# Rebuilding the stretch in front of the head loop of a Perceiver block's first cross-attention

## The reference, cut to what matters

```
xn = layernorm(layernorm(x)) * gamma + beta
q = (xn @ w_q).reshape(B, SQ, 16, 64)
k, v = jnp.split(context @ w_kv, 2, axis=-1)          # 12544 keys and values
scores = jnp.einsum('bqhd,bkhd->bhqk', q * SCALE, k)
attn = jax.nn.softmax(scores, axis=-1)
out = jnp.einsum('bhqk,bkhd->bqhd', attn, v).reshape(B, SQ, 1024)
x = x + (out @ w_out + b_out) * jnp.tanh(gate[0])
```

## Time and profile before

| | us |
|---|---|
| median of 3 runs (lowest, highest) | 1255.26 (1254.85, 1255.97) |
| the profiled execution, its own time | 1252.81 |
| its span, first to last instruction | 1251.0 |
| TensorE busy, share of the span | 1146.4, 92% |
| VectorE, ScalarE, GpSimd busy | 883.5, 861.5, 561.7 |

### The profile page before, as it was taken

One profiled execution on the slowest core, in us unless ns is written; L12 is line 12 of the kernel. 1 busy time (PEld: TensorE's weight loads), 2 busy tenths in 40 slices (PEclk: granted clock), 3 DMA queues, 4 the chain that ended last, 5 costly groups with the idle time before them and its releaser, 6 DMA issues. The chain is left out here.

```text
span 1251.0 us, 31264 instructions
## 1 busy us (share of the span) xinstructions
PE 1146.4 (92%) x12090; PEld 784.9 (63%) x12091; DVE 883.5 (71%) x1681; ACT 861.5 (69%) x1511; POOL 561.7 (45%) x532
## 2 busy tenths in 40 slices
PE   3699999999999999999999999999854989689698
PEld 1366666666666666666666666666642458534587
DVE  7777778887888888888787878787734641479522
ACT  2489988988888988889898888888830023294010
POOL 5055656565666565666565656565620000143000
PEclk9899999999999999999999999999985989889799
DMA  6155344544454444444444434444445727040264
GB/s 220 59 136 130 90 119 93 123 93 114 93 124 93 117 103 111 115 101 109 101 124 94 122 91 120 93 94 92 112 145 177 252 84 245 8 168 1 98 256 181
DMA packets 137741, 150.07 MB, mean 120 GB/s; under 512 B 17744, under 2 KB 125552, under 8 KB 137600
## 3 DMA queue, kind: packets, MB, share of 16 engines
q1 hardware_dynamic: 136784, 145.01, 42.8%
q10 hardware_dynamic: 816, 3.15, 0.7%
HBM read 72.25 MB, written 0.15 MB: 58 GB/s over the span
## 5 line engine op out<-in xcount | busy, mean ns | idle before, releaser
L430 POOL TENSOR_TENSOR pT_lo<-p_exp,pT_hi 128x896 f16<-128x896 f32 x223 | 420.9, 1888 | 334.2 <-ACT pT_hi L529 334.2
L510 ACT ACTIVATE p_exp<-ps,ln_k,esc 128x896 f32<-128x896 f32 x224 | 246.0, 1098 | 54.5 <-PE ps L859 46.7
L637 DVE TENSOR_REDUCE tile_max<-ps 128x128 f16<-128x896 f32 x224 | 244.5, 1092 | 50.1 <-PE ps L836 47.7
L529 ACT ACTIVATE pT_hi<-p_exp 128x896 f16<-128x896 f32 x224 | 211.7, 945 | 1.0
L632 DVE TENSOR_TENSOR v_lo<-ps,v_hi 128x512 f16<-128x512 f32 x196 | 135.6, 692 | 74.9 <-ACT v_hi L502 72.9
L877 PE MATMUL ps<-v_lo,pT_hi 128*128 128x64 f16 x1568 | 164.4, 193 | 0.0
L876 PE MATMUL ps<-v_hi,pT_hi 128*128 128x65 f16 x1568 | 164.3, 193 | 0.1
L823 PE MATMUL ps<-c_hi,wk_hi 128*128 128x448 f16 x448 | 158.9, 355 | 5.5 <-DVE k_st L713 3.6
L878 PE MATMUL ps<-v_hi,pT_lo 128*128 128x65 f16 x1568 | 163.8, 193 | 0.0
L823 PE MATMUL ps<-c_hi,wk_lo 128*128 128x448 f16 x448 | 158.5, 354 | 0.0
L823 PE MATMUL ps<-c_lo,wk_hi 128*128 128x448 f16 x448 | 158.5, 354 | 0.0
(11 more groups left out here) (331 smaller groups left out, 1914.1 us busy)
## 6 DMA issues: line engine op xcount, KB each, us to landing
k_st<-k_top SPq DMA_DIRECT2D x436, 112.0 KB, 2.3
k_st<-k_rest SPq DMA_DIRECT2D x436, 56.0 KB, 2.0
c_raw<-in_ctxT SPq DMA_DIRECT2D x14, 896.0 KB, 5.8
xa_ct<-in_ctxT SPq DMA_DIRECT2D x14, 896.0 KB, 4.7
xa_cn<-in_ctx SPq DMA_DIRECT2D x14, 896.0 KB, 5.2
me_w<-in_me_w SPq DMA_DIRECT2D x8, 1536.0 KB, 7.8
me_w<-in_me_w SPq DMA_DIRECT2D x8, 768.0 KB, 4.9
ss_c_all<-ss_bc SPq DMA_DIRECT2D x4, 512.0 KB, 5.3
```

What stands on the lines that cost most here:

```text
L430: nc.gpsimd.tensor_tensor(pT_lo[:, n % 2, :, :].rearrange("p t s -> p (t s)"), p_exp[:, n % 2, :], pT_hi[:, n % 2, :, :].rearrange("p t s ...
L510: nc.scalar.activation(p_exp[:, n % 2, :], s_scores[n % 2], ACT.Exp, bias=ln_k[:, 0:1], scale=esc[:, n // H0 % 2:n // H0 % 2 + 1]).then_in ...
L529: nc.scalar.activation(pT_hi[:, n % 2, :, :].rearrange("p t s -> p (t s)"), p_exp[:, n % 2, :], ACT.Copy).then_inc(pT_hi_ready, 1)
L637: nc.vector.tensor_reduce(tile_max[:, n % 2, :], s_scores[n % 2].rearrange("p (t s) -> p s t", s=S), AX.X, ALU.max).then_inc(tile_max_done, 1)
```

## The change

The time-ordered lists in front of the loop are rewritten; the loop and all later stages keep their instructions.

- Loads: `wv` moves from ScalarE's queue to SyncE's, ahead of `c_raw`; the six later loads move into the loop, to step 16 (`n == H0`).
- Fills: those of `k_st` and `q_low` are written as float32 words (two zeros, or two float16 minus ones, `MINUS_ONES`), so half as many elements; the rest of them come in another order. ScalarE waits for the first one only, VectorE for the ninth, and each user waits for what it needs. GpSimd pauses after the zeros until the normed x is ready.
- Queries: TensorE multiplies them before the bound; VectorE takes their largest value before the splits of `wk` and the context; ScalarE alone writes `q_twice`, and their PSUM banks are 2, 3, 6, 7.
- Value weights: GpSimd multiplies `wv` by its scale in place (two of 128x1024) and makes both `wv_lo` (VectorE did); ScalarE copies the high parts.
- Keys: only groups 0 and 1 (`K_DIRECT`) are written directly. Groups 2 to 5 go by `k_top`, `k_rest` and four DMAs each, as in the loop, and `first_pass(0)` stands behind group 3 on TensorE.

The diff, cut to its core:

```diff
...
+K_DIRECT = 2
...
-            return ps[:, (0, 1, 6, 7)[g], :].rearrange("p (h s) -> p h s", h=4)
+            return ps[:, (2, 3, 6, 7)[g], :].rearrange("p (h s) -> p h s", h=4)
...
                 sp.dma_start(x[:, :], a["x"]).then_inc(loaded["x"], 16)
                 sp.dma_start(rows[:, 0:R_BOUT, :], rows_dram[:, 0:R_BOUT, :].to_broadcast([P, R_BOUT, D])).then_inc(loaded["ln_rows"], 16)
+                sp.dma_start(wv[:, :, :], a["wv"].rearrange("(c p) n -> p c n", p=P)).then_inc(loaded["wv"], 16)
                 sp.dma_start(c_raw[:, :, :], ctxT[:, :, 0:CH]).then_inc(raw_loaded, 16)
-                sp.dma_start(rows[:, R_BOUT:, :], rows_dram[:, R_BOUT:, :].to_broadcast([P, NROWS - R_BOUT, D])).then_inc(loaded["rows"], 16)
-                sp.dma_start(gate[:, 0:1], a["gate"].to_broadcast([P, 1])).then_inc(loaded["rows"], 16)
-                sp.dma_start(cols[:, :], a["cols"]).then_inc(loaded["rows"], 16)
-                for n in ("wq", "wk", "wv"):
-                    sp.dma_start(ca_w[n][:, :, :], a["ca_" + n].rearrange("(c p) n -> p c n", p=P)).then_inc(loaded["ca"], 16)
...
-                for U in range(K_AHEAD):
+                for U in range(K_DIRECT):
                     for side in range(2):
...
                         sp.wait_ge(k_early_hi, 2 * U + side + 1)
...
+                def place_keys(U):
+                    b = U % 2
+                    at_least(sp, scores_done, 2 * (U // 2 - 4) + 2)
+                    sp.wait_ge(k_top_ready, U - K_DIRECT + 1)
+                    for side in range(2):
+                        r = DH * side
+                        sp.dma_start(k_st[(slice(r, r + DH),) + k_places(U, side)],
+                                     k_top[r:r + DH, b, :].unsqueeze(1).to_broadcast([DH, 2, HCH])).then_inc(k_placed[b], 16)
+                    sp.wait_ge(k_rest_ready, U - K_DIRECT + 1)
+                    for side in range(2):
+                        r, other = DH * side, DH * (1 - side)
+                        sp.dma_start(k_st[(slice(other, other + DH),) + k_place(U, side)], k_rest[r:r + DH, b, :]).then_inc(k_placed[b], 16)
+
+                for U in range(K_DIRECT, K_AHEAD):
+                    place_keys(U)
+
                 for n in range(NT):
                     c, h = n // H0, n % H0
+                    if n == H0:
+                        sp.dma_start(rows[:, R_BOUT:, :], rows_dram[:, R_BOUT:, :].to_broadcast([P, NROWS - R_BOUT, D])).then_inc(loaded["rows"], 16)
+                        sp.dma_start(gate[:, 0:1], a["gate"].to_broadcast([P, 1])).then_inc(loaded["rows"], 16)
+                        sp.dma_start(cols[:, :], a["cols"]).then_inc(loaded["rows"], 16)
+                        for m in ("wq", "wk", "wv"):
+                            sp.dma_start(ca_w[m][:, :, :], a["ca_" + m].rearrange("(c p) n -> p c n", p=P)).then_inc(loaded["ca"], 16)
                     if h == 8 and c + 2 < NCH:
                         sp.wait_ge(c_lo_ready, 4 * (c + 2))
...
                     U = n + K_AHEAD
                     if U < NT:
...
+                        place_keys(U)
...
+                        sp.wait_ge(w_ready, 2)
+                        sp.wait_ge(ones_ready, WV_LOW)
...
+                nc.gpsimd.memset(one[:, :], 1.0).then_inc(ones_ready, 1)
                 link(nc.gpsimd.memset(ident[:, :], 0.0))
...
+                nc.gpsimd.memset(un[:, 1:2], TINY).then_inc(ones_ready, 1)
+                nc.gpsimd.memset(ln_k[:, :], LN_K).then_inc(ones_ready, 1)
+                nc.gpsimd.memset(run_max[:, 1, :], -BIG).then_inc(ones_ready, 1)
                 nc.gpsimd.memset(v_hi[:, :, :, DH:VW], 1.0).then_inc(ones_ready, 1)
+                pool.wait_ge(ones_ready, 5)
+                nc.gpsimd.memset(k_st[DH:P, :, 0, 1, :].bitcast(F32), 0.0).then_inc(ones_ready, 1)
+                pool.wait_ge(ones_ready, 6)
+                nc.gpsimd.memset(k_st[0:DH, :, 1, 1, :].bitcast(F32), 0.0).then_inc(ones_ready, 1)
+                pool.wait_ge(ones_ready, 7)
+                pool.wait_ge(ident_ready, 1)
+                pool.wait_ge(shared["z_ready"], 1)
+                nc.gpsimd.tensor_copy(ident16[:, :], ident[:, :]).then_inc(ones_ready, 1)
+                nc.gpsimd.memset(q_low[:, :, :].bitcast(F32), 0.0).then_inc(ones_ready, 1)
+                pool.wait_ge(w_scale_ready, 2)
+                for c in range(DC):
+                    nc.gpsimd.tensor_scalar(wv[:, c, :], wv[:, c, :], w_inv[:, c:c + 1], None, ALU.mult).then_inc(ones_ready, 1)
+                pool.wait_ge(ones_ready, 11)
+                nc.gpsimd.memset(k_st[DH:DH + 1, :, 0, 1, :].bitcast(F32), MINUS_ONES).then_inc(ones_ready, 1)
+                pool.wait_ge(ones_ready, 12)
+                nc.gpsimd.memset(k_st[0:1, :, 1, 1, :].bitcast(F32), MINUS_ONES).then_inc(ones_ready, 1)
+                pool.wait_ge(ones_ready, 13)
+                nc.gpsimd.memset(tf_ones[:, :], 1.0).then_inc(ones_ready, 1)
                 nc.gpsimd.memset(acc[:, :, :], 0.0).then_inc(ones_ready, 1)
...
+                pool.wait_ge(c_lo_ready, 4)
+                for c in range(DC):
+                    pool.wait_ge(w_hi_ready, DC + c + 1)
+                    nc.gpsimd.tensor_tensor(wv_lo[:, c, :], wv[:, c, :], wv_hi[:, c, :], ALU.subtract).then_inc(ones_ready, 1)
...
-                act.dma_start(wv[:, :, :], a["wv"].rearrange("(c p) n -> p c n", p=P)).then_inc(loaded["wv"], 16)
                 act.dma_start(wq[:, :, :], a["wq"].rearrange("(c p) n -> p c n", p=P)).then_inc(loaded["wq"], 16)
-                act.wait_ge(ones_ready, 13)
+                act.wait_ge(ones_ready, 1)
...
+                def wv_high(c):
+                    act.wait_ge(ones_ready, WV_SCALED + c)
+                    nc.scalar.activation(wv_hi[:, c, :], wv[:, c, :], ACT.Copy).then_inc(w_hi_ready, 1)
+
+                wv_high(0)
                 for k in range(4):
                     c_high(0, k)
...
-                act.wait_ge(qn_done, 1)
                 act.wait_ge(q_scale_ready, 1)
...
+                for half in range(2):
+                    act.wait_ge(qn_done, half + 1)
+                    nc.scalar.activation(q_twice[half], ps[:, 2 + half, :].rearrange("p (h o e) -> p h o e", o=1, e=DH).to_broadcast([P, 8, 2, DH]),
+                                         ACT.Copy, scale=q_scale[:, 0:1]).then_inc(q_twice_ready[half], 1)
+                wv_high(1)
+
+                for U in range(K_DIRECT):
                     act.wait_ge(k_written, U + 1)
                     for side in range(2):
...
+                for g in range(4):
+                    act.wait_ge(q_done, g + 1)
+                    nc.scalar.activation(q_hi[:, 4 * g:4 * g + 4, :], q_bank(g), ACT.Copy).then_inc(q_hi_ready, 1)
+                for U in range(K_DIRECT, K_AHEAD):
+                    k_copy(U)
...
-                for k in range(DC):
-                    absmax(0, k)
...
                 nc.vector.tensor_scalar(w_inv[:, :], w_inv[:, :], W_TOP, None, ALU.mult).then_inc(w_scale_ready, 1)
-                v.wait_ge(ones_ready, 13)
+                for k in range(DC):
+                    absmax(0, k)
+                v.wait_ge(qn_done, 2)
+                link(nc.vector.tensor_reduce(q_abs[:, :], ps[:, 2:4, :], AX.XY, ALU.max, apply_absolute_value=True))
+                marks["q_abs"] = link.count
+                v.wait_ge(ones_ready, Q_LOW_ZERO)
                 scale(0)
+                v.wait_ge(q_max_done, 1)
+                link(nc.vector.tensor_reduce(q_un[:, :], ps[:, 0, 0:P], AX.X, ALU.max))
+                link(nc.vector.tensor_scalar(q_un[:, :], q_un[:, :], 1.0 / Q_TOP, TINY, ALU.mult, ALU.max))
+                nc.vector.reciprocal(q_scale[:, :], q_un[:, :]).then_inc(q_scale_ready, 1)
                 v.wait_ge(w_scale_ready, 2)
...
-
                 for k in range(4):
                     c_low(0, k)
...
+                for U in range(K_DIRECT):
                     for side in range(2):
...
+
+                def queries_low(g):
+                    v.wait_ge(q_hi_ready, g + 1)
+                    for side in range(2):
+                        r, hs = slice(DH * side, DH * side + DH), slice(4 * g + side, 4 * g + 4, 2)
+                        nc.vector.tensor_tensor(q_low[r, hs, :], q_bank(g)[r, side:4:2, :], q_hi[r, hs, :], ALU.subtract).then_inc(q_ready, 1)
+
+                queries_low(0)
+                queries_low(1)
+                k_low(2)
                 tiles_max(0)
+                queries_low(2)
+                k_low(3)
                 new_max(0)
-                for k in range(DC):
-                    absmax(1, k)
+                queries_low(3)
+                for U in range(4, K_AHEAD):
+                    k_low(U)
                 for vn in range(TILES):
                     v_low(vn, 0, 0, vn)
+                    if vn < DC:
+                        absmax(1, vn)
                 tiles_max(1)
...
-                    if U < K_AHEAD:
+                    if U < 4:
```

(37 more changed lines are left out.)

88 lines of the change are left out of this document (7 added, 81 removed).

## The result

The changed kernel took 1250.62 us (median of 20 runs, 1247.87 to 1253.95). The kernel before, run beside it, took 1254.96 (20 runs, 1250.26 to 1256.13). The ratio is 0.9972, with a 95% interval of 0.9961 to 0.9983: 3.5 us faster by the ratio (4.3 by the two medians), with 1250.8 forecast. The profiled execution took 1248.33 and had a span of 1246.2, 4.8 less than that of before.

A forecast was written before the change was run, and what follows sets the result against it. TensorE bounds the loop, and mostly VectorE's instruction list the stretch until the first value product. 8.6 - 2.2 (clock) - 0.9 (contention) - 1.0 (loads) = 4.5 us sooner: 1250.8 us, 8-in-10 range 1246.5 to 1254.2.

The forecast's parts named there:

- Norm and fills: Start of the kernel: fills as words end before z, saving 2.0 us; norm ready at 10.05 instead of 12.08.
- Loads: Start: wq there at about 11.6, wv at 12.6, weight scales at 16.1, about 5 us sooner.
- q_scale 21.08 (20.8), group 0 at 24.82 (24.5): Ahead of the loop: q_scale at 20.8, 9.4 us sooner; key group 0 can start at 24.5, 4.7 sooner.
- The new wait: k_top of group 5 waits for group 3's buffer until 37.9; value products start at 39.1, 8.6 us sooner.
- Clock, 2.2: Key groups 0 and 1: twelve TensorE steps at half clock after idling cost 2.2 us; bounds 0 and 4.
- Contention, 0.9: Splits wk_lo and c_lo on VectorE slowed by GpSimd's work beside them: 0.9 us, a third of 2.7.
- GpSimd's value weights, 0: GpSimd's products on wv and rests, ahead of the value products: no cost; list ends at 40 at worst.
- From the first value product to `turn_max`, 14.5 carried over: Stretch just ahead of the loop: taken as unchanged from before, 14.5 us.
- Six loads, 1.0: Loop step 16: loads ahead of group 22's placing on SyncE cost 1.0 us; bounds 0 and 3.9.
- The rival on a stalled loop: Six loads delay group 22's placing some 12 us; ScalarE and TensorE stand 8 us; 1257.8, slower by 2.5; chance 6%.
- the under 2 that I had named: Sign in the loop: a wait of ScalarE at step 16 to 18 of under 2 us.
- The sum of 4.5: Whole kernel: 8.6 us from the head less 2.2, 0.9 and 1.0 gives 4.5 us sooner.

The follow-up runs named there:

- the 21 products: Changed kernel with 21 unused TensorE products added in the wait ahead of key group 0: 1253.58 us in one run.
- Four buffers: Changed kernel with four buffers of k_top and k_rest instead of two, and a semaphore for each: 1242.62 us, ratio 0.9914.
- the second profile: The changed kernel run again without edits, as base for the other runs: 1250.89 us, ratio 0.998.
- the run with the late scale: Changed kernel with query maximum and queries' scale put behind the four remainders of the context's first half on VectorE: 1251.88 us in one run.
- the 12 products: Changed kernel with 12 unused TensorE products added in the wait ahead of the loop's first turn_max: 1253.65 us, ratio 0.9995.

## Why the prediction was right

Step by step, in its order:

- **Norm and fills: right.** `z` and `y` at 0.41; x itself landed 0.4 later than in before, so the norm was at 10.46 and not 10.05. Putting the fills back cost 1.4 us at the first value product, not the 2.0, since VectorE waited 0.5 and 0.9 us for `wv` in the two profiles of the changed kernel and not at all with the old fills.
- **Loads: right.** Queries at 11.96 (11.6), `wv` landed at 13.1 (12.6), weight scales at 16.42 (16.1).
- **q_scale 21.08 (20.8), group 0 at 24.82 (24.5): right,** 0.3 late throughout.
- **The new wait: right in place and nearly in size.** From group 0 to the first value product it was to be 14.6 us with a fast array, and with the 21 products it was 14.67 (24.69 to 39.36); here it was 15.63 with the cold steps in it. Four buffers show that it was the path, and that it cost 2.1 us there.
- **Clock, 2.2: right mechanism, oversized.** Nine of twelve steps were slow, where I had taken all; they cost 1.5 us where they stand and 1.0 at the first value product (15.63 against 14.67). In the second profile eleven were slow, 2.0 there and 1.4 at the first value product. The slow weight loads of the queries were read rightly against the listed 1.00 of that stretch. By the rule of the Trainium skill (TensorE: Matmul & The Clock Gate, What's actually happening) that an array falls back when idle and rises when kept busy, both runs with added products ahead of group 0 agree: full clock only where they filled the wait. (The wait ahead of the loop doesn't decide by itself, see below.)
- **Contention, 0.9: not there.** `wk_lo` 2.48 and `c_lo` 2.47, as before. The Trainium skill (SBUF — State Buffer, SBUF: two separate sides) says that a VectorE instruction with two SBUF inputs is held up only by a GpSimd one that reads SBUF. For the fills the traces agree: `wk_lo` and `c_lo` ran beside them unhindered, so this would have been the better term for them. For GpSimd's products on `wv`, which read, they don't bear it out: by the same section the one that comes second stands still until the first is done, but here the first `wk_lo` started at 21.00, 1.2 us ahead of the end of the product (22.20), and took its usual 1.28. In the run with the late scale one `wk_lo` beside such a product took 2.08 and the next, some 0.7 us of it beside the same product, 1.27. The cause of that one delay stays open. I took a third of the loop's slowdown for want of looking at which GpSimd instruction stood where.
- **GpSimd's value weights, 0: right.** Products 2.84 us each, rests 2.11 each, done at 30.9.
- **From the first value product to `turn_max`, 14.5 carried over:** 15.06.
- **Six loads, 1.0: 1.9 measured,** inside the bounds of 0 and 3.9. (The rival on a stalled loop reckoned with 8.5 us for two steps; they take 7.7, 861.3 us for 223.) The wait of 2.1 us is just above the under 2 that I had named. I read the slack from a stretch with one load ahead of a placing; here the DMA engines' busy share, in the kernel's second profile, was 0.85 to 1.11 from 124 to 130 us.
- **Not in the sum:** the loop's first group at half clock, 1.4 lost (shown by the 12 products), and 2.1 won back along the loop, 0.4 ahead of the six loads and 1.6 behind them. That it was won back from waits of before, of which its trace has 5.2 us for `k_rest` and this one 4.0 with the six loads' wait in it, fits, and wasn't tested by itself.
- **Not tested:** the order of the loads of `wq` and `wv`, and the placing of groups 2 to 5 by DMA without the new order around it. What was undone one at a time (fills 1.4, queries' order 2.8, value rests 0.2, six loads 0.4 at most) comes to 4.8 of the 7.3 us at the first value product.

For the first value product the terms said 39.1 + 2.2 + 0.9 = 42.2, and it came at 40.45: 1.75 us better, and then 0.5, 1.4 and 0.9 worse, 2.1 better in the loop, 0.7 worse behind it. The sum of 4.5 met 4.8 in the trace and 4.3 (1254.96 - 1250.62) in the medians. So the total was met more closely than its terms, by errors that cancelled, and that was luck; what was right is the path.
